# Attention of a layered transformer kernel on one Trainium2 core: VectorE's subtraction for Q's low part moved to the end of its step, query products seven units ahead, three sets of rotated queries

## The reference, cut to what matters

```
q = _rmsnorm(x @ wq_a.T, q_a_ln_w) @ wq_b.T
q_nope, q_pe = (q[..., :NOPE], q[..., NOPE:])
...
q_pe = _apply_rope(_deinterleave(q_pe), cos, sin)
...
scores = jnp.einsum('bqhd,bkhd->bhqk', q_full, k_full) * softmax_scale
scores = jnp.where(causal[None, None], scores, jnp.finfo(scores.dtype).min)
attn = jax.nn.softmax(scores, axis=-1)
out = jnp.einsum('bhqk,bkhd->bqhd', attn, v).reshape(B, S, H * VD)
return out @ wo.T
```

## Time and profile before

| | us |
|---|---|
| median of three runs | 1893.45 |
| the three runs | 1893.23, 1893.45, 1898.54 |
| the profiled execution, its time | 1889.85 |
| its span, first to last instruction | 1888.1 |

### The profile page before, as it was taken

The page is one execution under the profiler, slowest core; times in us unless marked ns, Lnnn a source line. Parts: engine busy times, 40 slices in busy tenths (PEclk is TensorE's granted clock), DMA queues, the critical chain, the costliest instruction groups (busy, mean ns, idle before and its releaser), DMA issues. The chain is left out here.

```text
span 1888.1 us, 32153 instructions
## 1 busy us (share of the span) xinstructions
PE 1628.8 (86%) x12482; PEld 967.1 (51%) x12482; DVE 1033.8 (55%) x2772; ACT 881.5 (47%) x1670; POOL 809.4 (43%) x705
## 2 busy tenths in 40 slices
PE   6896699997877888888888888858999999579998
PEld 5564355554444555555555555543444444245564
DVE  5697457774767777777777777754110000244343
ACT  4774322222647888888888888853000000231110
POOL 3222244444636777777777777750000000133441
PEclk9898799998999999999999999978999999789999
DMA  9773424544425778778787877769533321333322
GB/s 313 229 241 125 128 56 125 160 118 112 90 45 107 152 153 155 157 149 154 141 163 148 155 149 143 141 146 274 138 90 65 92 45 23 107 75 71 89 68 79
DMA packets 556568, 244.04 MB, mean 129 GB/s; under 512 B 502016, under 2 KB 532736, under 8 KB 556032
## 3 DMA queue, kind: packets, MB, share of 16 engines
q1 hardware_dynamic: 556416, 241.98, 54.9%
HBM read 67.88 MB, written 48.23 MB: 61 GB/s over the span
## 5 line engine op out<-in xcount | busy, mean ns | idle before, releaser
L1574 ACT ACTIVATE xb<-D_S,D_sv,qw_c 128x512 f32<-128x512 f32 (+3 forms) x512 | 285.9, 608 | 127.5 <-DVE D_sv L1635 127.5
L1689 POOL TENSOR_TENSOR xb<-xb 128x1280 f16<-128x1280 f32 x128 | 335.1, 2618 | 12.2 <-ACT xb L1582 12.2
L48 PE MATMUL F_o<-F_wh,N_hT 128*128 128x384 f16 (+1 forms) x768 | 257.5, 335 | 6.5 <-DVE F_wl L899 6.5
L49 PE MATMUL F_o<-F_wl,N_hT 128*128 128x384 f16 (+1 forms) x768 | 257.4, 335 | 0.0
L50 PE MATMUL F_o<-F_wh,N_hT 128*128 128x384 f16 (+1 forms) x768 | 257.1, 335 | 0.0
L92 POOL TENSOR_SCALAR mv<-mv 128x1 f32<-128x1 f32 x64 | 26.7, 417 | 507.2 <-DVE mv L87 506.2
L1628 DVE TENSOR_REDUCE D_sv<-D_S 128x1 f32<-128x512 f32 (+3 forms) x512 | 224.5, 479 | 2.7 <-PE D_S L1533 2.7
L48 PE MATMUL E_o<-E_mh,E_ot 128*128 128x512 f16 x512 | 195.6, 382 | 15.5 <-DVE E_ml L1797 11.3
L1524 PE MATMUL D_S<-kTh,D_QTh 128*128 128x512 f16 (+3 forms) x512 | 156.1, 305 | 50.6 <-ACT xb L1574 50.4
L50 PE MATMUL E_o<-E_mh,E_ot 128*128 128x512 f16 x512 | 195.8, 382 | 0.0
L49 PE MATMUL E_o<-E_ml,E_ot 128*128 128x512 f16 x512 | 195.8, 382 | 0.0
(11 more groups left out here) (212 smaller groups left out, 3649.9 us busy)
## 6 DMA issues: line engine op xcount, KB each, us to landing
A_wo<-in_wo SPq DMA_DIRECT2D x16, 1024.0 KB, 6.1
od<-D_os SPq DMA_DIRECT2D x32, 512.0 KB, 3.1
mwd<-A_mst SPq DMA_DIRECT2D x32, 256.0 KB, 2.4
xd<-xb SPq DMA_DIRECT2D x16, 512.0 KB, 4.0
E_rm<-mwd SPq DMA_DIRECT2D x16, 512.0 KB, 4.8
xb<-xd SPq DMA_DIRECT2D x16, 512.0 KB, 6.1
out_x<-xb SPq DMA_DIRECT2D x16, 512.0 KB, 2.9
xb<-in_x SPq DMA_DIRECT2D x6, 1024.0 KB, 19.6
```

The source lines that it names most:

```text
L48: e.matmul(out, a[0], b[0], start=start, stop=False, **kw)
L49: e.matmul(out, a[0], b[1], start=False, stop=False, **kw)
L1574: m = e.activation(p[:, AT[i]:AT[i] + N], Sb[n % 4][:, c:c + N], ACT.Exp, scale=qw.col(qw.NEG, g), bias=s[:, 7 - i:8 - i])
L1689: e.tensor_tensor(P2[u % 3][:, 1280:2560], P[u % 3][:, :], P2[u % 3][:, 0:1280], ALU.subtract).then_inc(s_pl, 1)
```

## The change

Three things are changed in `attention`, none of them an instruction's size:

1. In VectorE's step `low_q(u+2)` goes behind `bias(u, 1)` and so to the end; `least(u, 2)` goes ahead of `normalize(u-5)`.
2. AQ goes from 6 to 7: query, nope, rotate and add_q run one unit further ahead of the scores.
3. `qs` has three sets in place of two, and ScalarE's `nope(u)` waits for the turned queries of the set used three groups of four earlier (`4 * (u // 4 - 2)`) in place of two.

```diff
-    qs = [ph.sb(f"qs{i}", [128, 4, 4, 128]) for i in range(2)]
+    qs = [ph.sb(f"qs{i}", [128, 4, 4, 128]) for i in range(3)]
...
-    AQ, LAG = 6, 5
+    AQ, LAG = 7, 5
...
-            w.wait_ge(s_t, 4 * (u // 4 - 1))
-            e.activation(qs[u // 4 % 2][:, tt, :, 0:64], pn, ACT.Copy, scale=QSCALE).then_inc(s_qn, 1)
+            w.wait_ge(s_t, 4 * (u // 4 - 2))
+            e.activation(qs[u // 4 % 3][:, tt, :, 0:64], pn, ACT.Copy, scale=QSCALE).then_inc(s_qn, 1)
...
             if there(u + AQ - 1):
                 rotate(u + AQ - 1)
+            if there(u):
+                least(u, 2)
             if there(u - LAG):
                 normalize(u - LAG)
             if there(u):
-                least(u, 2)
+                bias(u, 1)
             if there(u + 2):
                 low_q(u + 2)
-            if there(u):
-                bias(u, 1)
```

More of the change, by code:

```diff
@@ L1501, in turn_q @@
             g, b, h = units[u]
-            ps, q = t_bank("t", u), qs[u // 4 % 2]
+            ps, q = t_bank("t", u), qs[u // 4 % 3]
             w.wait_ge(s_qn, 4 * (u // 4) + 4)
@@ L1649, in rotate @@
             pp = qb[u % 2][:, 256:512].rearrange("p (h d) -> p h d", h=4)
-            qv, m = qs[u // 4 % 2][:, tt, :, :], t2b[u % 2]
+            qv, m = qs[u // 4 % 3][:, tt, :, :], t2b[u % 2]
             def wide(ap, n):
```

## The result

| | before | after |
|---|---|---|
| median, us | 1893.34 (four runs, 1891.77 to 1898.54) | 1953.40 (four runs, 1950.05 to 1961.20) |
| profiled execution, us | 1889.85 | 1953.73 |
| its span, us | 1888.1 | 1951.9 |

The ratio of after to before is 1.0318, with a 95% interval of 1.0282 to 1.0355. The forecast was 1958 us, in a range from 1942 to 1984.

The account below looks back on a forecast made before the run. Loop B, 5.45 us a step through low_p and the held bias1, was taken to bind. Terms +70.2, +0.5, -4.5 and -1.5 sum to +64.7 on 1889.85: 1954.6, or 1958 us on the median's scale; range 1942 to 1984.

Parts of the forecast that it names:

- Loop B: Second attention: bias0, add_q, low_p, held bias1, two smallest-of-row instructions, bias0 again; 5.45 us, said to bind the kernel before.
- Loop A: Second attention: high_q, low_q, bias1, exps, high_p and back to high_q; 5.42 us, 0.03 short of binding.
- The new step: Units 5 to 121: low_q's 0.60 us, hidden before, lengthens the step to 6.05 us; 117 steps add 70.2 us.
- The hold: VectorE's bias1, SBUF to SBUF, stands still until GpSimd's low_p ends, released at +3.30 us; chance 0.74.
- The first rival: Bias1 is not held by low_p: step falls to TensorE's 4.50 us, total 1776 us; chance 0.14.
- AQ 7: Queries one unit further ahead: worth nothing in a 6.05 us step; one more query product first costs +0.5 us.
- a fall of the clock: TensorE idles 1.55 us per step and drops to 1.2 GHz for over half of it: 1976 us; chance 0.08.
- The start and the end: Units 1 to 4, without normalize, run at about 4.6 us: -4.5 us; from unit 122, without add_q: -1.5 us.

Follow-up runs that it names:

- the versions without a long hold: Changed kernel with bias1 ahead of normalize, 1772.29 us; changed kernel with each bias as two single-column instructions, 1766.80 us.
- the order alone: Changed kernel with AQ back at 6, two sets and the old wait in nope, keeping only VectorE's new order: 1964.16 us.
- the versions with six units ahead: AQ 6 and two sets: kernel before 1893.34 us; changed kernel put back to these 1964.16 us; that with bias1 ahead of normalize 1810.15 us.

## Why the prediction was right

**The binding loop.** Right. Loop B, through low_p and bias1, gave 5.45; halving low_q left the step at 5.445. Loop A, put at 5.42, was measured by opening loop B: 5.509 with a pair of biases that takes 0.10 longer, so 5.41.

**The new step.** Forecast 6.05, measured 6.040; bias1's arrival at +0.91 and its release at +3.30 stand in the trace to 0.02. 117 x 0.593 = 69.4 against 70.2.

**The hold.** Right. The rows of the kernel before showed it by themselves, with biases that end 0.02 to 0.03 us behind low_p. The Trainium skill names such a hold for a tensor_scalar in a two-port mode, and for an instruction with two SBUF inputs beside a GpSimd instruction that reads SBUF (SBUF — State Buffer, "Who interferes with whom"). The runs agree on both: 2.41 us and 2.40 us. The first rival put the step without a hold at 4.50 us and the total at 1776; the versions without a long hold came in at steps of 4.51 and 4.50, and at 1772 and 1767 us. It was right about its number, and its condition did not come: bias1 found low_p 0.23 us under way in all 117 steps.

**AQ 7.** Here the forecast failed. I took it for worth nothing in a step of 6.05, since the wait before the turn lay in PE's spare time. I had its length from the old order (up to 1.7 us) and did not work it out for the new one, where PE reaches the turn 2.8 us ahead of add_q; and I named a fall of the clock as a rival for the idle time before the scores, not for this wait. With the order alone the clock did fall, and 10 us were lost that AQ 7 saved. The total was not hurt, since AQ 7 is in the change. At the start it helped as well: the kernel before has one step of 6.86 us there, with a wait of 2.7 us before the turn and a lower clock behind it (0.93 over these four steps), which with seven units ahead is gone.

**The start and the end.** These were mis-sized. From the attention's first query product to bias0 of unit 5 I had put -4.5 and +0.5, in sum -4.0; it was -6.3. The head start of one query shows as 0.2 (19.7 against 19.5 us to bias0 of unit 1), less than the versions with six units ahead differ among themselves there (18.9 to 19.8). What was off is the rest. The four steps behind it were put at 4.6 and ran in 4.18: ACT, busy for 16.6 of their 16.7 us, bounds them and has no high_o there yet, which the 4.6 had left in. The bias slipped in between add_q and low_p, as assumed from the one place where a waiting bias was seen to get in. The end was -3.0 against -1.5, with four steps of 4.97 and one of 4.37 where I had taken 4.93 as the lower bound for each. All terms together were put at +64.7 and measured at +60.1, which is also the difference of the medians. That the two profiled executions differ by 63.9, so near to 64.7, is luck: 3.7 of it lie outside this attention.

**The clock.** At 6.04 the clock stayed at the 2.4 GHz level (1.00), with 1.3 us of idle in each step. That rival did not come. Its 3.4 us at the lower level in each step stood in no row. Its other assumption, that work takes twice as long there, is what the rows of the order alone show (0.42 against 0.22 us between matmuls).

## What to carry to other kernels

When an instruction is moved, work out at what moment of the other engines' step it arrives, and not only what it waits for by semaphore: VectorE instructions that go from SBUF to SBUF can stand still for a whole GpSimd instruction, even where they take 0.23 us by themselves; here only those of a single column did not. Such a stall is shown as busy time, so look at the largest duration of each line beside its median, and compare the busy time of one engine between two kernels with the same instructions. Where two loops have nearly one length, a change that opens only one of them shows nothing or a loss; test it together with the one that opens the other.

## What the runs showed of the hardware that I had not expected

- A tensor_scalar of 128x1 float32 in SBUF is not held by GpSimd (202 to 216 ns in all 512 cases), one of 128x2 is (2.41 us). The pair takes 0.33 us where the single one takes 0.23 unheld, so it costs 0.10 and saves the hold. Other widths, odd ones among them, were not run, so what it is about one column that avoids the hold stays open.
- A VectorE instruction that waits for GpSimd is let in between two GpSimd instructions that stand one behind the other (bias1 ended 0.02 us behind the first half of low_p, the second half ran on at once). GpSimd showed no loss by it. It has to be there in time: 0.11 us before the end was enough, 0.10 us was not, and it then waited for the next instruction too.
- Waits of TensorE with different outcomes: 1.3 us in each step of 6.04 left the clock in full; 29 waits of up to 1.7 us in the kernel before did too; with the order alone, 29 waits of 2.6 to 2.8 us, one in every fourth step, came 15 times with a fall to the lower level at their end or within 1.4 us behind it, and 14 times without.
